# Attention scores from two float32r parts on row halves in place of three bf16 parts, in a kernel with three attentions on one Trainium2 core

## What is computed

```python
# layer 0: cross attention on 77 context tokens
x = softmax(Q(x) K(c)^T / 4) V(c) + x              # "A0"
# layer 1
q, k, v = split(layernorm(x) @ sa_in_w.T + sa_in_b)
x = x + merge(softmax(q k^T / 4) v) @ sa_out_w.T + sa_out_b     # "A1", 1024 keys
cq, ck, cv = layernorm(x) @ cq_w.T + cq_b, c @ ck_w.T + ck_b, c @ cv_w.T + cv_b
x = x + merge(softmax(cq ck^T / 4) cv) @ co_w.T + co_b          # "A2", 77 keys
x = x + gelu(layernorm(x) @ w1.T + b1) @ w2.T + b2              # 1024 wide
```

## Time and profile before

| | |
|---|---|
| time of three runs, us | 838.48 median (835.05 to 842.11) |
| the profiled execution, first to last instruction, us | 836.5 |
| PE busy | 749.0 (90%), 4182 matmul records |
| DVE busy | 530.3 (63%) |
| ACT busy | 452.1 (54%) |
| POOL busy | 164.8 (20%) |
| maxima in A1, L949 on DVE | 303.0, 256 of 1220 ns |
| exponentials, L843 on ACT | 346.2, 640 of 598 ns |
| PV, L742 on PE | 174.8, 1280 records of 619 ns |
| ST, L728 on PE | 204.7, 598 records of 391 ns |
| maxima's matmuls in A1, L675 on PE | 153.2, 512 of 383 ns |
| maxima's matmuls in A0 and A2, L680 on PE | 41.8, 512 of 212 ns |
| chain that ended last | PE 72%, DMA 11%, DVE 7%, ACT 4% |

### The profile page before, as it was taken

One profiled execution on the slowest core, in us unless ns is written; L12 is line 12 of the kernel. 1 busy time (PEld: TensorE's weight loads), 2 busy tenths in 40 slices (PEclk: granted clock), 3 DMA queues, 4 the chain that ended last, 5 costly groups with the idle time before them and its releaser, 6 DMA issues.

```text
span 836.5 us, 11551 instructions
## 1 busy us (share of the span) xinstructions
PE 749.0 (90%) x4182; PEld 338.4 (40%) x4224; DVE 530.3 (63%) x836; ACT 452.1 (54%) x826; POOL 164.8 (20%) x355
## 2 busy tenths in 40 slices
PE   6677896589999999999999999997989897999998
PEld 3333444235222222222333333332444453556767
DVE  3445978475888888888878878874457767140001
ACT  4355553245776777777666666666644645422120
POOL 7312362364000000000000101223123214030000
PEclk9779899698999999999999999999999999999999
DMA  8967515992014060511406001004261730000001
GB/s 268 187 176 130 124 41 147 120 163 74 2 23 56 1 77 2 64 15 24 54 1 77 2 2 23 20 21 90 48 155 48 143 45 2 1 1 25 26 13 38
DMA packets 43769, 52.82 MB, mean 63 GB/s; under 512 B 9344, under 2 KB 29760, under 8 KB 43712
## 3 DMA queue, kind: packets, MB, share of 16 engines
q1 hardware_dynamic: 43424, 51.99, 32.7%
q10 hardware_dynamic: 288, 0.08, 0.1%
HBM read 36.31 MB, written 15.15 MB: 62 GB/s over the span
## 4 chain that ended last, share of the span: by engine, by line
PE 72%; DMA 11%; DVE 7%; ACT 4%; issue 3%; SPq 2%; POOL 1%; another core or an unknown queue 0%; ACTq 0%; DVEq 0%; POOLq 0%
PE PV L742 18%; PE ST L728 15%; PE SM L675 12%; PE ST L641 5%; PE ST L637 5%; DMA stacks<-mrow 3%; DMA stacks<-q_parts 3%; DVE nm L949 3%; PE SM L628 3%; PE SM L618 2%; DMA q_parts<-split 2%; PE SM L622 2%; PE PV L641 2%; PE PV L637 2%; PE SM L680 2%
## 5 line engine op out<-in xcount | busy, mean ns | idle before, releaser
L843 ACT ACTIVATE prob<-ST 128x512 f32<-128x512 f32 (+1 forms) x640 | 346.2, 598 | 180.9 <-PE ST L728 152.0
L949 DVE TENSOR_REDUCE nm<-SM 128x1 f32<-128x1024 f32 x256 | 303.0, 1220 | 65.4 <-PE SM L675 64.2
L728 PE MATMUL ST<-stacks 128*128 128x512 bf16 (+1 forms) x598 | 204.7, 391 | 20.7 <-DMA stacks<-mrow 13.9
L742 PE MATMUL PV<-prob,Vst 128*32 128x512 f32 x1280 | 174.8, 619 | 3.1 <-ACT prob L843 2.8
L675 PE MATMUL SM<-stacks 96*128 96x512 bf16 x512 | 153.2, 383 | 23.0 <-DMA stacks<-q_parts 14.3
L728 PEld LDWEIGHTS ST<-stacks 128*128 128x128 bf16 (+1 forms) x640 | 57.1, 101 | 206.6 <-ACT prob L843 141.7
L952 DVE TENSOR_REDUCE nm<-SM 128x4 f32<-128x308 f32 x128 | 58.3, 473 | 47.9 <-PE SM L680 47.2
L675 PEld LDWEIGHTS SM<-stacks 96*128 96x128 bf16 x512 | 47.9, 98 | 80.6 <-DVE nm L949 20.1
L1116 POOL CAST mp<-nm 128x16 bf16<-128x16 f32 x48 | 9.6, 199 | 356.3 <-DVE nm L949 249.2
L905 DVE TENSOR_TENSOR X<-ST,X 128x256 f32<-128x256 f32 x18 | 7.5, 423 | 90.5 <-PE ST L641 73.7
L742 PEld LDWEIGHTS PV<-prob,Vst 128*32 128x32 f32 x1280 | 25.5, 109 | 62.8 <-ACT prob L843 34.7
(11 more groups left out here) (102 smaller groups left out, 674.3 us busy)
## 6 DMA issues: line engine op xcount, KB each, us to landing
stacks<-q_parts SPq DMA_DIRECT2D x144, 128.0 KB, 5.7
q_parts<-split SPq DMA_DIRECT2D x24, 384.0 KB, 4.3
stacks<-k_parts SPq DMA_DIRECT2D x48, 128.0 KB, 7.5
k_parts<-split SPq DMA_DIRECT2D x8, 384.0 KB, 3.8
fm<-in_xT SPq DMA_DIRECT2D x4, 512.0 KB, 7.9
X<-in_x SPq DMA_DIRECT2D x4, 512.0 KB, 5.2
V<-in_w SPq DMA_DIRECT2D x2, 1024.0 KB, 9.0
out<-X SPq DMA_DIRECT2D x16, 128.0 KB, 1.7
```

Source lines behind the costliest of these rows:

```text
L728: mm(ST[0:att.keys, n % 3, :], keys_of(att, g, h, kt), QST[att.name][g % att.buffers][:, h, j * BLK:(j + 1) * BLK], start=True, stop=True) \
L742: last = mm(PV[h * 32:(h + 1) * 32, :], Vst[:, g % 2, kt, h, :], prob[:, t % 2, h, :], start=(kt == 0), stop=(kt == att.kt - 1))
L843: act_fn(prob[0:att.keys, t % 2, h, :], ST[0:att.keys, n % 3, :], ACT.Exp) \
L949: ins = vec.tensor_reduce(nm[:, q % 2, v // QUAD, v % QUAD:v % QUAD + 1], ps, AX.X, ALU.max, negate=True)
```

## The change

Queries and keys are split into two float32r parts in place of three bf16 parts. Three bands of 16 rows carry the products (high x high, high x low, low x high), then two rows with the parts of the negative maximum, which meet ones. That is 50 rows, so two heads lie side by side: even heads in rows 0 to 63, odd ones in 64 to 127 (`HALF`), and a matmul works on one half. The bands have as many bytes as before, in rows of 4 KB in place of 2 KB. The unused rows of Q are filled with zeros from SBUF at every stack (two more transfers of 128 KB each), those of K with ones by POOL. The scale of the scores goes into the exponential.

ACT writes the high part out of PSUM with the bias and DVE the low part out of PSUM; q32, r32 and POOL's share go. A "max" unit in A1 is now two heads against 512 keys, and the two halves of the keys are joined at the end of each q (`na`); in A0 and A2 it is two tiles of queries, four heads, 78 columns each (the last key is doubled). The rows of a q need one transpose, and go out in four transfers of 4 KB, one for each head. PE runs heads in pairs, and PV comes after the fourth head. Side results use two halves of SM everywhere. The stored parts are 512 KB per chunk in place of 384. The hidden layer of the feed-forward moves from the stacks to `prob` and to the weights' space. The core of the diff:

```diff
-PARTS = 3
-BANDS = [(0, 0), (0, 1), (0, 2), (1, 0), (1, 1), (2, 0)]
+PARTS = 2
+PAIR = QUAD // 2
+CTXP = CTX + 1
+HALF = P // 2
+BANDS = [(0, 0), (0, 1), (1, 0)]
 SROWS = len(BANDS) * HD
 MROWS = SROWS + PARTS
-TWO_ONES = float(np.array([0x3F803F80], np.uint32).view(np.float32)[0])
 SB = 4
+SIDES = 2
...
-        self.units = TPB * (QUAD if self.whole else 1)
+        self.units = TPB * PAIR * (SEQ // BLK) if self.whole else TPB // 2
...
+                if g == 0:
+                    sp.wait_ge(pad_ready, 3 if att is A1 else 1)
                 heads = slice(g * QUAD * HD, (g + 1) * QUAD * HD)
+                for side in range(2):
+                    rows = slice(side * HALF + SROWS, (side + 1) * HALF)
+                    sp.dma_start(QST[att.name][n][rows, :, :].bitcast(FP32).rearrange("p n (c t) -> p (n c) t", t=BLK),
+                                 zeros[:, :].unsqueeze(1).to_broadcast([HD, PAIR * HALVES, BLK])) \
+                      .then_inc(stack_in[att.name][n], 16)
                 for band, (kpart, qpart) in enumerate(BANDS):
-                    rows = slice(band * HD, (band + 1) * HD)
-                    if att.whole:
-                        sp.dma_start(Kst[n][rows, :, :],
-                                     KP[att.name][kpart, heads, :].rearrange("(h d) t -> d h t", d=HD)) \
+                    for side in range(2):
+                        rows = slice(side * HALF + band * HD, side * HALF + (band + 1) * HD)
+                        if att.whole:
+                            sp.dma_start(Kst[n][rows, :, :].bitcast(FP32), KP[att.name][kpart, heads, :]
+                                         .rearrange("(n s d) t -> s d n t", s=2, d=HD)[side]) \
+                              .then_inc(stack_in[att.name][n], 16)
+                        sp.dma_start(QST[att.name][n][rows, :, :].bitcast(FP32), QP[att.name][qpart, heads, :]
+                                     .rearrange("(n s d) t -> s d n t", s=2, d=HD)[side]) \
                           .then_inc(stack_in[att.name][n], 16)
-                    sp.dma_start(QST[att.name][n][rows, :, :],
-                                 QP[att.name][qpart, heads, :].rearrange("(h d) t -> d h t", d=HD)) \
-                      .then_inc(stack_in[att.name][n], 16)
...
-                    sp.dma_start(QST[att.name][g % att.buffers][SROWS:MROWS, :, j * BLK:(j + 1) * BLK],
-                                 mrow[:, q % 2, :]).then_inc(rows_in[q % 2], 16)
+                    for c in range(QUAD):
+                        side, n = divmod(c, PAIR)
+                        rows = slice(side * HALF + SROWS, side * HALF + MROWS)
+                        sp.dma_start(QST[att.name][g % att.buffers][rows, n, j * BLK:(j + 1) * BLK].bitcast(FP32),
+                                     mrow[c * PARTS * TPB:(c + 1) * PARTS * TPB, q % 2, :].bitcast(FP32)) \
+                          .then_inc(rows_in[q % 2], 16)
...
                     if att.whole:
-                        h = v % QUAD
-                        for c in range(SEQ // BLK):
-                            last = mm(ps[:, c * BLK:(c + 1) * BLK], Q[0:SROWS, h, c0:c0 + P],
-                                      Kst[g % att.buffers][0:SROWS, h, c * BLK:(c + 1) * BLK],
-                                      start=True, stop=True)
+                        tile, n, c = v // 4, v // 2 % 2, v % 2
+                        c0 = j * BLK + tile * P
+                        for s in range(2):
+                            rows = slice(s * HALF, (s + 1) * HALF)
+                            last = mm(ps[:, s * BLK:(s + 1) * BLK], Q[rows, n, c0:c0 + P],
+                                      Kst[g % att.buffers][rows, n, c * BLK:(c + 1) * BLK], start=True, stop=True)
...
-                    for n in range(TPB):
-                        last = nc.tensor.transpose(ps.bitcast(BF16)[0:PARTS * QUAD, n * P:(n + 1) * P],
-                                                   mp[:, which % 2, n].rearrange("p r h -> p (r h)"), identb[:, :])
+                    last = nc.tensor.transpose(ps[:, 0:P], mp[:, which % 2, :].bitcast(FP32), ident[:, :])
...
+                    rows = slice(h % 2 * HALF, (h % 2 + 1) * HALF)
                     mm(ST[0:att.keys, n % 3, :], keys_of(att, g, h, kt),
-                       QST[att.name][g % att.buffers][:, h, j * BLK:(j + 1) * BLK], start=True, stop=True) \
+                       QST[att.name][g % att.buffers][rows, h // 2, j * BLK:(j + 1) * BLK], start=True, stop=True) \
...
-                    for h in range(QUAD):
-                        if t < att.steps:
+                    for n in range(PAIR):
+                        for h in range(2 * n, 2 * n + 2) if t < att.steps else []:
                             scores(t, h)
+                        if n == 1 and 1 <= t <= att.steps:
+                            values(t - 1)
                         for slot, w in work:
-                            if slot == h:
+                            if slot // 2 == n:
                                 side(att, w)
-                        if h == 1 and 1 <= t <= att.steps:
-                            values(t - 1)
...
-                act_fn(split[:, n % SB, 0, 0:width], q32[:, n % SB, 0:width], ACT.Copy).then_inc(part1_ready, 1)
-            def second_part(w):
-                n, width = CHUNK[w], width_of(w)
-                act.wait_ge(*REST[n])
-                act_fn(split[:, n % SB, 1, 0:width], r32[:, n % SB, 0:width], ACT.Copy).then_inc(part2_ready, 1)
+                act_fn(split[:, n % SB, 0, 0:width], ps[:, 0:width], ACT.Identity, bias=cols[:, c:c + 1]) \
+                    .then_inc(high_ready, 1)
...
+                        if pair == 1 and q is not None:
+                            values_out(att, q)
+                        for slot, w in att.side(t):
+                            if slot // 2 == pair and w[0] in SPLITS:
+                                act.wait_ge(*side_in_bank(w))
+                                high(w, side_bank(att, w))
...
-                    if n >= SB:
-                        dve.wait_ge(*REST[n - SB])
-                    return vec.tensor_scalar(q32[:, n % SB, 0:width], ps[:, 0:width], SPLITS[stage][3],
-                                             cols[:, c:c + 1], ALU.mult, ALU.add)
+                    dve.wait_ge(high_ready, n + 1)
+                    return vec.scalar_tensor_tensor(split[:, n % SB, 1, 0:width], ps[:, 0:width], cols[:, c:c + 1],
+                                                    split[:, n % SB, 0, 0:width].bitcast(FP32), ALU.add, ALU.subtract)
...
+                if kind == "max" and v == att.units - 1:
+                    halves = [nm[:, q % 2, c].rearrange("p i (n s) -> p s n i", s=2) for c in range(2)]
+                    dve.wait_ge(*READ[w])
+                    by_side = na[:, q % 2].rearrange("p (s n) i -> p s n i", s=2)
+                    if att.whole:
+                        ins = vec.tensor_tensor(by_side, halves[0], halves[1], ALU.min)
+                    else:
+                        ins = vec.tensor_copy(by_side, halves[0])
+                    ins.then_inc(max_ready, 1)
...
-                a, r, m = nm[:, q % 2], nr[:, q % 2], mp[:, q % 2]
-                gp.tensor_copy(m[:, :, 0, :], a).then_inc(mp_p1, 1)
-                pool.wait_ge(mp_p1, n + 1)
-                gp.tensor_tensor(r, a, m[:, :, 0, :], ALU.subtract).then_inc(mp_r1, 1)
-                pool.wait_ge(mp_r1, n + 1)
-                gp.tensor_copy(m[:, :, 1, :], r).then_inc(mp_p2, 1)
-                pool.wait_ge(mp_p2, n + 1)
-                gp.tensor_tensor(m[:, :, 2, :], r, m[:, :, 1, :], ALU.subtract).then_inc(mp_ready, 1)
+                a, m = na[:, q % 2], mp[:, q % 2, 0:TPB * PARTS * QUAD].rearrange("p (c r i) -> p c r i", c=QUAD, r=PARTS)
+                gp.tensor_copy(m[:, :, 0, :], a).then_inc(mp_high, 1)
+                pool.wait_ge(mp_high, n + 1)
+                gp.tensor_tensor(m[:, :, 1, :], a, m[:, :, 0, :].bitcast(FP32), ALU.subtract).then_inc(mp_ready, 1)```

How the order moves, at three places. PE, plain steps of A1, before (ST are the scores, SM the maxima, PV the values; `x4` for PV are four matmuls):

```order
L742 MATMUL PV<-prob,Vst 32x512 x4
L728 MATMUL ST<-stacks 128x512 x2
L675 MATMUL SM<-stacks 128x512 x2
L728 MATMUL ST<-stacks 128x512 x2
L675 MATMUL SM<-stacks 128x512 x2
L742 MATMUL PV<-prob,Vst 32x512 x4
```

328 lines of the change are left out of this document (125 added, 203 removed).

## The result

| | before | after |
|---|---|---|
| median, us | 838.88 (835.05 to 842.11) | 915.43 (911.34 to 920.17) |
| ratio | | 1.0932, interval 1.0879 to 1.0985 |
| profiled span, us | 836.5 | 914.2 |
| mean granted clock | 0.961 | 0.901 |

A forecast was written before the change was run, and what follows sets the result against it. It took PE work alone to bound A1 before, and a 2.65 us loop through the exponential and PV after. Terms -10 - 4 + 7 + 4 + 8 + 9 = +14 on the 836.5 span gave 850.5, median 852; range 820 to 888.

The forecast's parts named there:

- -10 and -4: A1: 10 us saved where nothing runs under it, 4 us saved with products under it and at its end.
- not side by side: Rival: row halves do not run side by side, or two passes; A1's loop 2.86, 884 us in all; chance 0.20.
- full rate: Rival: float32r matmuls run at the full float32 rate, 4.65 us an A1 step, 1100 us in all; chance 0.05.
- Fourth ST 0.22: A1's loop: the step's fourth ST, after the exponential and hand-over and ahead of PV, takes 0.22 us of 2.65.
- 0.04 for weights that load in 0.19 and not 0.10: A1's loop: slower weight loads add 0.04 us to the step's 2.65.
- 0.50 and 0.04 between: A1, once per q: each of four row issues costs 0.50 us with 0.04 between, 2.1 together.
- 1.0 to land: A1, once per q: the rows' transfer lands 1.0 us after the issues, making rows 0.7 late (0.4 to 1.6).
- 3.70 becomes 2.65 + 0.86 + 0.10: A1 with products under it: the new length in us of a step that holds a product.
- Sum 3.74: A0 and A2: a plain step's loop adds up to 3.74 us, +0.27 on 3.47 for 16 steps, +4.
- 8 us, where two steps give 7.5: A0: SP's queue per group, 8 stack issues and 8 of rows at 0.5, against two steps' time.
- By piece: Rival: transfers cost by piece, not by port; 128 KB takes 0.54 us, 817 us in all; chance 0.20.
- rows in time: Rival: issues at 0.3, so rows are not late; A1 -11, A2 -4, 837 us in all; chance 0.12.

The follow-up runs named there:

- e6: The changed kernel with both max units of an A1 step put ahead of the third head: 888.67 us, ratio 1.0612.
- e3: The changed kernel with A1's rows made one step earlier (rows_at 5 for 6): 894.41 us, ratio 1.0663.
- e2: The changed kernel with PV, and ACT's copy of PV, behind the second head again: 895.47 us, ratio 1.0652.
- b1: The kernel before with PV, and ACT's copy of PV, behind the fourth head in place of the second: 848.05 us, ratio 1.0137.
- e1_full: The changed kernel plus one unused float32 matmul of 128 columns on all 128 rows per max unit of A0 and A2: 913.47 us, ratio 1.0897.
- e5: The changed kernel without zero fills, scores on 50 rows and maxima on 48, plus e1_full's added matmul: 939.45 us, ratio 1.1202.
- e9: e8 plus e1_full's added matmul in the max units of A0 and A2: 908.94 us, ratio 1.0849.
- e1_half: The changed kernel with e1_full's added matmul on rows 0 to 63 alone: 921.78 us, ratio 1.0987.
- e12: e11 without the added matmul, that is e8 with one of four rows transfers left in A0 and A2: 908.88 us, ratio 1.0845.
- e11: e9 with one of four rows transfers left in A0 and A2, maxima of three heads in four left out there: 899.72 us, ratio 1.0738.
- e8: The changed kernel with each zero fill cut from 16 rows to two, matmuls still on 64 rows: 909.15 us, ratio 1.0870.
- h0: The kernel before with the change in A1 alone, A0 and A2 keeping three bf16 parts and their order: 855.36 us, ratio 1.0225.
- v2: The changed kernel with the edits of e8, e3 and e6 together: 861.50 us, ratio 1.0296.

## Why the prediction was wrong, point by point

**Where the 64 us are.** The span grew by 77.7 and not by 14. A1 has 42 of the difference (+14.8 and +13.1 for -10 and -4): its loop and the late rows were priced too low, and PV's move under products not at all. A0 and A2 have 29 (+24.1 and +22.3 for +8 and +9): their steps were added up at full clock. The preamble and the stretch ahead of A1 gave 8 back.

**A1's matmuls: right in kind.** One pass, pairs side by side, PE no longer the bound, the loop through the exponential with PV in it. The rivals "not side by side" and "full rate" fell: two SM matmuls of 512 columns take 0.43 with their exposed weight load, and four take 0.52 (e6).

**A1's loop, the first step that failed: one term mis-sized.** "Fourth ST 0.22" and "0.04 for weights that load in 0.19 and not 0.10" gave 2.65. The ST that waits for the exponential loads its weights only then, 0.18, and PV starts 0.49 after it; that alone is 0.23 of the 0.25 missing a step. The other pieces came within 0.1 and cancel (SM pair and turn 0.43 for 0.32, ST to its exponential 0.32 for 0.43). Over 128 steps 0.25 is 32 us, 17 of them in the first nine q. The row for it stood in the earlier trace rows: a weight load behind the exponential. The prediction added the difference of two weight loads where the whole load lies on the path. The Trainium skill, TensorE: Matmul & The Clock Gate, Weight-path perf modes — Fast Weight Load (FWL) and DoubleRow, keeps the quick load to types other than FP32; the trace's 0.18 to 0.19 for float32r against 0.10 for bf16 fits that, and the page is silent on float32r.

**Rows late: right, too small.** "0.50 and 0.04 between" and "1.0 to land" were 0.61 to 0.67 and 1.73, so 1.6 late and not 0.7 (e3), at the edge of "0.4 to 1.6". Over 16 q that is 14 us more. With the loop: 23.0 + 2.0 + 0.9 is the 25.9 measured for a q.

**PV's place: not costed.** The text put PV into the loop but gave its move no price under products, where "3.70 becomes 2.65 + 0.86 + 0.10". e2 shows 13.6 us there and 10.5 in A2, b1 6 and 6 within A1 of the kernel before. The "-4" also left out the 0.3 that each q gains in the first part's sum, 2 us. The loop, the rows and PV's place are why it became +13.1; how the three share it is not shown, and e2's sizes come from its quickest execution.

**A0 and A2: the second step that failed.** "Sum 3.74" took every piece at full clock, and the text named a falling clock only for A1, where it hardly fell. In A0's first ten steps the clock was the bound: 6.40 a step at 0.50, PE without a gap. At full clock the sum was about right: e1_full's 4.28 less its two added matmuls of 0.21 is 3.86, by estimate. In A2 the clock fell less, 0.86 for 0.96, and its length goes with it (120 us at 0.82 in e3, 107 at 0.94 in e2). Row-half matmuls had replaced matmuls over 96 and 128 rows there. That fewer rows lower the clock is shown in A1 (e5 against e9), and that added float32 work raises it in A0 (e1_full); that the rows are why it fell in A0 and not in A1 is argued, and three things speak against it as the whole reason. PV, "rows" and "out", all over 128 rows, are 3.31 of the 6.40, more than PV's 1.00 of 2.90 in A1; the matmul on half of the rows raised the clock too (e1_half), and so did PV's place alone (e2). Why A0 fell and A1 did not stays open. The queue term, "8 us, where two steps give 7.5", was right in kind and 9.0 in size; it lay under the slow PE (e12) and is the second bound once that goes (e9, e11). With both lifted (e11) A0 and A2 take 215.1 together, 12 less than in the change and 35 more than before; no run here says what those 35 are. The Trainium skill, TensorE: Matmul & The Clock Gate, What's actually happening, says that the gate follows how busy the PE has been. Here PE's records were busy for all of 54 to 109 us at 1.2 GHz; the measurement decides, and the page does not mention rows.

**Preamble and the stretch ahead of A1.** +4.4 and -1.0 for +7 and +4. The fills' price could not be shown: e8 cut them by seven eighths and neither stretch got shorter. "By piece" and "rows in time" did not happen as rivals: the rows were late (e3), and from 166 to 176 us, with the DMA engines full of stacks and fills, 129 GB/s were moved, about 1.0 us for 128 KB and not 0.54. The shorter splitting may have brought more than its -3: h0, with three full fills, took 4 off there, while stores of float32r parts landed later, one in 16.6 us (189.18 to 205.8) for 12.70 in the earlier trace rows.

**Tail.** Unchanged, as said.

## What to carry to other kernels

Count a weight load that waits for the same release as its matmul in full. Ask of every stage that gets narrower matmuls what the granted clock will do, and not only of the stage that the change is for; no rule found here tells which stage will fall, so read it from a first trace. A change that pays in one stage can be made there alone: the parts in A1 alone, with two small edits of order, are 3% faster than the kernel before; in all three attentions they are 9% slower, and 3% slower with the same two edits and small fills (v2).

## What the hardware showed that was not expected

- PE can be busy without a gap at a granted clock of 0.50 (A0, 54 to 109 us). And in A1 the granted clock was 1.00 with scores and maxima on 64 rows of each half (e9, 225 to 300 us) and 0.88 with them on 50 and 48 (e5), with the same columns and order.
- A plain float32 matmul of 128 columns on all rows, twice a step, brought A0's steps from 0.50 to 1.00, in e1_full by 66 us, in e9 and e11 only by 90; on half of the rows it did so in parts. PV two heads earlier, with nothing added, did so in parts too (e2).
- A float32r matmul of 512 columns takes one pass; its weights load in 0.18 to 0.19 (bf16 0.10), unhidden behind a wait and behind PV.
- An issue of 4 KB from SBUF to SBUF costs SP 0.61 to 0.67, one of a band of 128 KB 0.42: the small transfer costs the queue more.
